# Where a small expert tile's transposes stand in the TensorE queue, and where a pair's last hidden part is split

## The reference

```python
    def _L0_ffn_ref(x, Wr, Wg, Wu, Wd):
        ...
        logits = jnp.einsum('bsh,he->bse', x, Wr)
        probs = jax.nn.softmax(logits, axis=-1)
        topk_w, topk_idx = jax.lax.top_k(probs, TOP_K)
        topk_w = topk_w / jnp.sum(topk_w, axis=-1, keepdims=True)
        ...
        cw = jnp.zeros((T, E), dtype=x.dtype).at[jnp.arange(T)[:, None], idxf].add(wf)
        gate = jax.nn.silu(jnp.einsum('th,ehi->tei', xf, Wg))
        hidden = gate * jnp.einsum('th,ehi->tei', xf, Wu)
        out = jnp.einsum('tei,eih,te->th', hidden, Wd, cw)
```

## Time and profile before

| | |
|---|---|
| median of 3 executions | 880.22 us (879.32 to 880.75) |
| the profiled execution | 879.26 us, of it 877.5 us span |
| PE busy | 93% of the span |
| DVE busy | 78% |
| ACT busy | 72% |
| POOL busy | 42% |

### The profile page before, as it was taken

One profiled execution on the slowest core, in us unless ns is written; L12 is line 12 of the kernel. 1 busy time (PEld: TensorE's weight loads), 2 busy tenths in 40 slices (PEclk: granted clock), 3 DMA queues, 4 the chain that ended last, 5 costly groups with the idle time before them and its releaser, 6 DMA issues.

```text
span 877.5 us, 19817 instructions
## 1 busy us (share of the span) xinstructions
PE 812.4 (93%) x6049; PEld 767.2 (87%) x6049; DVE 686.9 (78%) x1637; ACT 634.6 (72%) x1980; POOL 367.8 (42%) x531
## 2 busy tenths in 40 slices
PE   5998999999999999429999999999999999999993
PEld 4846899999999998329999999999999999999993
DVE  7667888888898778674787877878788787878771
ACT  3557898898889887235777777777777787777771
POOL 3021377687688667600332322333222334334322
PEclk9999999999999999858999999999999999999998
DMA  8044801410400204644253623666446445555312
GB/s 290 2 132 148 256 31 38 134 38 26 145 32 32 86 26 136 232 103 126 43 140 100 187 46 77 178 165 160 133 103 188 102 92 133 150 140 137 57 25 24
DMA packets 78732, 96.41 MB, mean 110 GB/s; under 512 B 10343, under 2 KB 66083, under 8 KB 78627
## 3 DMA queue, kind: packets, MB, share of 16 engines
q1 hardware_dynamic: 63955, 76.07, 28.5%
q0 software_dynamic: 13584, 18.03, 11.3%
q10 hardware_dynamic: 1088, 1.06, 0.5%
HBM read 117.19 MB, written 31.42 MB: 169 GB/s over the span
## 4 chain that ended last, share of the span: by engine, by line
PE 84%; DMA 5%; SPq 4%; DVE 3%; issue 2%; ACT 1%; DVEq 0%; POOL 0%; POOLq 0%; ACTq 0%
PE banks L311 25%; PE banks L312 24%; PE banks L313 24%; PE banks L1241 4%; PE banks L1379 2%; DMA valmat_dram<-val_st 2%; PE banks L1312 2%; PE banks L1173 1%; SPq L554 1%; DMA expert_in<-blank 1%; PE banks L1209 1%; DMA valmat_dram<-late_f 1%; PE banks L1197 1%; PE banks L1224 1%; DMA wkv_sb<-in_L_xattn_Wkv 0%
## 5 line engine op out<-in xcount | busy, mean ns | idle before, releaser
L863 POOL DMA_INDIRECT result<-res,tok_id x73 | 120.4, 1649 | 201.2 <-ACT res L1070 183.5
L311 PE MATMUL banks<-tok_t_hi,wgt_hi 128*128 128x256 f32 x704 | 201.9, 287 | 2.9 <-DVE tok_t_lo L1773 2.8
L312 PE MATMUL banks<-tok_t_lo,wgt_hi 128*128 128x256 f32 x704 | 200.3, 285 | 0.0
L313 PE MATMUL banks<-tok_t_hi,wgt_lo 128*128 128x256 f32 x704 | 200.3, 285 | 0.0
L1789 DVE TENSOR_TENSOR wgt_lo<-wgt,wgt_hi 128x704 fp32r<-128x704 f32 (+1 forms) x192 | 165.7, 904 | 19.3 <-ACT wgt_hi L1028 19.1
L961 ACT ACTIVATE prob<-banks,row_min 128x77 f32<-128x77 f32 x512 | 161.6, 375 | 3.4 <-DVE row_min L1577 3.4
L1028 ACT ACTIVATE wgt_hi<-wgt 128x704 fp32r (+3 forms) x192 | 143.9, 801 | 18.0 <-DVE wgt_lo L1768 11.1
L311 PEld LDWEIGHTS banks<-tok_t_hi,wgt_hi 128*128 128x128 f32 x704 | 135.8, 193 | 5.2 <-DVE wgt_lo L1789 3.1
L312 PEld LDWEIGHTS banks<-tok_t_lo,wgt_hi 128*128 128x128 f32 x704 | 135.9, 193 | 0.0
L313 PEld LDWEIGHTS banks<-tok_t_hi,wgt_lo 128*128 128x128 f32 x704 | 135.9, 193 | 0.0
L961 ACT ACTIVATION_READ_ACCUMULATOR prob<-banks,row_min 128x1 f32 x512 | 131.4, 259 | 0.0
(11 more groups left out here) (249 smaller groups left out, 2137.2 us busy)
## 6 DMA issues: line engine op xcount, KB each, us to landing
wgt<-in_L_ffn_Wg SPq DMA_DIRECT2D x33, 704.0 KB
wgt<-in_L_ffn_Wu SPq DMA_DIRECT2D x33, 640.0 KB
wgt<-in_L_ffn_Wd SPq DMA_DIRECT2D x33, 640.0 KB
tok<-expert_in SPq DMA_DIRECT2D x32, 258.0 KB
single_wgt<-in_L_ffn_Wg SPq DMA_DIRECT2D x9, 704.0 KB
single_wgt<-in_L_ffn_Wu SPq DMA_DIRECT2D x9, 640.0 KB
single_wgt<-in_L_ffn_Wd SPq DMA_DIRECT2D x9, 640.0 KB
valmat_f<-valmat_dram SPq DMA_DIRECT2D x4, 1197.0 KB, 6.3
```

The lines of the kernel that those rows point to most:

```text
L311: nc.tensor.matmul(to, a[0], b[0], start=first, stop=False)
L312: nc.tensor.matmul(to, a[0], b[1], start=False, stop=False)
L313: return nc.tensor.matmul(to, a[1], b[0], start=False, stop=last)
L863: nc.gpsimd.indirect_dma_start(out, bass.IndirectOffsetOnAxis(ap=tok_id[i][:, a:a + 1], axis=0), res[i][:, a, :], None, compute_op=ALU.add ...
```

## The change

Two edits, on four engines' programs. In the pair's last unit (u = 2) the hidden values are rounded by ACT and split by DVE before the two pieces of the next tile's weights, no longer behind them. In a single's step PE puts `hid_turn` between the two halves of the pair's down products, no longer behind both; and ACT rounds the single's turned hidden values before it moves the pair's result.

```diff
@@ ACT, pair_step @@
                 for u in range(UNITS):
                     silu(t, u)
+                    if u == UNITS - 1:
+                        hid_round(t, u)
                     if ahead:
                         round_pieces(t + 1, u, src)
-                    hid_round(t, u)
+                    if u < UNITS - 1:
+                        hid_round(t, u)
...
@@ ACT, single_step @@
+                single_hid_round(t)
                 res_move(t - 1)
-                single_hid_round(t)
                 if not last:
                     round_pieces(t + 1, 2, src)
...
@@ PE @@
-            def down(t):
+            def down(t, between=None):
...
                         mm = nc.tensor.matmul(to, h[0][:, FC - 1, :], x[:, FC - 1, :], start=False, stop=x is w[1])
+                    if between is not None and not a:
+                        hid_turn(between)
                 mm.then_inc(down_done, 1)
...
-                down(t - 1)
-                hid_turn(t)
+                down(t - 1, between=t)
...
@@ DVE, pair_step @@
                     hidden(t, u)
+                    if u == UNITS - 1:
+                        hid_rest(t, u)
                     if ahead:
                         rest_pieces(t + 1, u, src)
-                    hid_rest(t, u)
+                    if u < UNITS - 1:
+                        hid_rest(t, u)
```

## The result

| | kernel before | changed kernel |
|---|---|---|
| median of the runs | 879.6 us (10 runs, 877.1 to 880.8) | 883.8 us (10 runs, 882.5 to 887.0) |
| ratio to before | | 1.0053, 95% interval 1.0039 to 1.0068 |
| span of the profiled execution | 877.5 us | 881.5 us |

A forecast was written before the change was run, and what follows sets the result against it. DVE's chain through a single's step was taken to bound the kernel, though PE is busiest: 8 x (0.65 - 0.21 = 0.44) + 0.2 = 3.7 us on 880.22 gives 883.9 us, own range 882.8 to 885, whole range 881.0 to 886.2.

The forecast's parts named there:

- What bounds: Through a single's step DVE is the limit; PE, busy 93%, already waits about 0.1 us at the next pair's `gate_up`.
- The first stall: PE's wait before the pair's first down product, for DVE's last hidden rest: 0.81 us per single, removed by the change.
- The shift: DVE's `single_hid` and last gate and up piece come 1.52 - 0.87 = 0.65 us later, delaying the next `gate_up`.
- Transposes between the halves: In a single's step PE waits some 0.35 us for `single_hid` there, at no net cost.
- The pair behind: The pair after a single regains 0.21 us, with 0.3 us or more of slack, leaving 0.44 us net per single.
- The third stall: PE's wait for split tokens at the end of the pair behind a single, 0.21 us; expected to go away.
- The other pairs: 22 steps without a single: DVE ends 0.65 us later, covered by its idle time of 1.8 us each.
- The end: At the last single the last down matmul starts 0.2 us later; the single's sooner down products buy nothing.
- The sum: Whole kernel: 8 x 0.44 + 0.2 = 3.7 us added to a median of 880.22, giving 883.9 us, slower by 0.4%.
- Faster: Rival, chance 0.08: PE keeps its gain, all three stalls go, 1.1 us at eight singles, 9 us: 871 us.
- The third stall stays: Rival slower than forecast, chance 0.12: split-token wait remains in the pair behind, 8 x 0.65 + 0.2 = 5.4 us, 885.6 us.
- No measurable change: Rival, chance 0.16: DVE's delay is half as large (881.5 us), or the end gains its 2.5 us (881.4 us).

The follow-up runs named there:

- the two pieces moved out: A single's two down weight pieces split behind the next pair's four gate and up pieces, against the kernel before: 874.15 us, 0.9947.
- the halves swapped: Changed kernel, but in the pair's last unit DVE multiplies the half on partitions 64 to 127 first, the whole block second: 883.04 us, 1.0059 to the kernel before.
- A: The hidden part ahead of the weight pieces on ACT and DVE; alone at every pair, on the kernel before: 882.77 against 878.45 us, 1.0049.
- B: Single's transposes between the halves of `down`, its rounding ahead of `res_move` on ACT; without the hidden part's move, on the kernel before: 878.48 us, 0.9998.
- the kernels that moved the two pieces: Four kernels splitting a single's down pieces behind the next pair's gate and up pieces, against the kernel before: 874.15, 871.45, 871.13 and, the last, 870.12 us.
- the end kept: Late down pieces, but at the last single transposes behind both halves and ACT moving the pair's result first, against the kernel before: 871.45 us, 0.9922.

## Why the prediction was right

*What bounds.* Right. DVE's chain from the pair's last product to the next pair's last weight piece sets a single's step: 0.91 us out of it took 0.90 us off the step with all of PE's work in place, and with the two pieces moved out PE went on without a pause.

*The first stall goes and brings nothing.* Right: 1.37 to 0.55 us at the place, with 1.16 us of wait at `gate_up` (1.1 to 1.2 expected). From the first product to `gate_up` it is 497.00 - 487.46 = 9.54 us, against 9.44 expected and 8.79 before. ACT's idle time of 0.92 us ahead of its rounding was 0.9 in the prediction. By starts PE stands 8 x 0.82 = 6.6 us less at the first place and 8 x (1.16 - 0.1 + 0.47) = 12.2 us more at the two new ones, where 6.5 and 12 were expected.

*The shift.* The mechanism was right, its term was too small: 0.65 us in the sum, 0.745 measured per step. The waits that I counted are there: ACT's weight pieces start 1.52 us behind DVE's first product (488.98 - 487.46), where they started with it before, and DVE's have moved by 1.52 too. What I had wrong is the 0.87 us that I took off for L1824 and L1825. It ran to the start of `single_hid`, which began 0.02 us behind the end of L1825 before, where an instruction without a hold begins about 0.08 us ahead of that end (494.77 + 0.68 = 495.45, against 495.37 for the next). So by these rows about 0.10 us of the 0.87 was no work of L1825 but a hold of `single_hid`, and it came along behind the weight pieces; in the kernel before this wasn't tested. With the halves swapped it is gone, and the step grew by 0.62.

*Transposes between the halves.* Right that they cost nothing in a single's step: without A they left it at 20.28, and with A it is 21.03 against 21.04. The wait was 0.47 us, not 0.35, for the same held instruction; with the halves swapped it is 0.34 (492.71 - 492.25, less 0.12). At the last single they are not free: A alone shortens the end by 1.19 us, and B gives 1.57 back. The prediction's working of the end had both in one figure, so it didn't see that the change was better off without B there.

*The pair behind.* Right only in part. The third stall shrank to 0.06 us (0.42 us over three matmuls against 0.56, with 0.36 usual) where I had 0.3 us or more of slack, and the pair gained 0.12 us and not 0.21. DVE's and PE's timelines in that pair:

```profile
500.81 0.69 DVE L1801 TENSOR_TENSOR hid_f<-gate_act,banks 128x512 f32<-128x512 f32 x1 [0.71 <-ACT gate_act L1035]
501.60 1.69 DVE L1793 TENSOR_TENSOR wgt_lo<-wgt,wgt_hi 128x704 fp32r<-128x704 f32 x2
...
506.69 0.68 DVE L1777 TENSOR_TENSOR tok_t_lo<-banks,tok_t_hi 128x512 fp32r<-128x512 f32 x1
```

```profile
507.25 0.28 PE L312 MATMUL banks<-tok_t_lo,wgt_hi 128*128 128x256 f32 x1
...
507.67 0.28 PE L312 MATMUL banks<-tok_t_lo,wgt_hi 128*128 128x256 f32 x1
```

DVE now waits 0.71 us for the silu there, and its weight piece comes 0.79 us behind the product's start, where a product without a wait behind it took 0.60 (504.13 to 504.73 in the kernel before); I had DVE go on without a pause. DVE's token rest still ends at 506.69 + 0.68 = 507.37, when PE's weight load for the next matmul would be due; it came at 507.45. That this is the whole of the difference wasn't tested.

*The other pairs.* Right: +0.03 us in fourteen steps, and +0.02 with A at those alone. Their cover, DVE's idle time of the earlier trace rows, shrank to 36.9 us and was enough.

*The end.* 0.2 us predicted, 0.38 measured. The timeline of the last single:

```profile
857.40 0.42 DVE L1803 TENSOR_TENSOR hid_f<-gate_act,banks 128x256 f32<-128x256 f32 x1 [1.41 <-ACT gate_act L1038]
...
862.53 0.55 DVE L1817 TENSOR_TENSOR single_hid<-single_act,banks 128x384 f32<-128x384 f32 x1
...
865.77 0.28 PE L1382 MATMUL banks<-wgt_lo,hid_hi 128*128 128x256 f32 x1
```

The single's values start 5.13 us behind the first product, 0.74 more than before (858.17 - 853.78 = 4.39), in place of 0.65. The pair's last down matmul starts 8.37 us behind it, against 861.81 - 853.78 = 8.03, so 0.34 us is there. The single's own result was ready for ACT 2.6 us sooner (10.72 us behind the first product, 13.30 before), and bought nothing, as forecast. The chain ends as the prediction has it, on the pair's second output DMA:

```profile
869.56 3.66 DMA result<-res,tok_id
873.22 0.27 issue
873.49 1.55 POOL result L863
```

*The sum.* By steps the loss is 5.5 us in the two profiles where the prediction had 3.7, and 4.7 (3.4 to 6.0) by the ratio of the times. That the forecast of 883.9 us meets the 883.8 measured is partly chance: I added 3.7 us to a median of 880.22, which later runs put at 879.6, and from there the same sum gives 883.3.

*The rivals.* "Faster" fell, but its condition was named rightly: it wants DVE's chain short, and the kernels that moved the two pieces came near its 9 us (8 us in the last). "The third stall stays", 5.4 us, came close in its sum with another cause. "No measurable change" fell in both its forms: the shift was not half but more than the whole of mine, and the end grew by 0.38 us and gained nothing.

## What to carry to other kernels

A gap on the busiest engine says where its spare time falls, not what limits it: before you close it, look at the next place where that engine meets the same partner, and at how much slack it has there (here none: PE's weight load began 0.06 us behind DVE's last piece). Reordering inside the limiting engine's chain lost here, because it put a round trip between two engines into it; at the other pairs, where DVE stood idle anyway, the same order cost nothing. What won was to take out of the chain the work that nobody needs yet (here two pieces wanted a step later, worth 0.5%, and 0.8% with the end kept). And a closeness of totals isn't a proof: the forecast met the measured time within 0.1 us, while its sum, read step by step, was a third too small.

## What the runs showed of the hardware

- An instruction on DVE that reads PSUM from partition 0, behind a last reader that began on partition 64, started 0.10 us later than with a last reader that began on partition 0 (1.85 against 1.75 us), even with four instructions on SBUF in between.
- Loading the tile table's numbers into DVE's registers cost no time that shows (1.85 us with and without it in front).
- Once in the expert part of each of the fourteen profiles, between 793 and 808 us, POOL pauses between a pair's two scattered adds for 2.6 to 6.7 us, with nothing that the profile names. In the kernel with the end kept, its timeline:

```profile
793.66 1.70 POOL L878 DMA_INDIRECT result<-res,tok_id  x1 [4.79 <-issue]
797.58 1.22 POOL L870 COPY tok_gate<-tok 128x1 f32<-128x1 f32 x1 [2.22 <-DMA result<-res,tok_id]
```

The copy behind the pause is what the load of the next tokens waits for (it is issued at 801.34), so this made the tokens late. The kernel before has such a pause too, of 4.07 us ahead of the add at 800.63, without a wait of PE behind it; the cause is open.
